# A graph layer's two sums put into one stage, with maxima, tally and stores of counts in the first sum's pass

## What is computed

```
_spmm(edge_src, edge_dst, edge_val, dense):
    msgs = dense[edge_src] * edge_val[:, None]
    return segment_sum(msgs, edge_dst, num_segments=N_NODES)

h1  = relu(_spmm(src, dst, edge_weight, y) @ W1 + b1)     # y: x after a normalization
out = elu (_spmm(src, dst, edge_weight, h1) @ W2 + b2)
x   = x + out
```

## Time and profile before

| | us |
|---|---|
| median of three runs | 3237.06 (3233.52 to 3242.03) |
| the profiled execution | 3245.63 |
| its span, first to last instruction | 3243.9 |
| first-sum stage, from its first transfer's issue | 451.7 to 838 |
| second-sum stage | 838 to 1171 |

### The profile page before, as it was taken

One profiled execution on the slowest core, in us unless ns is written; L12 is line 12 of the kernel. 1 busy time (PEld: TensorE's weight loads), 2 busy tenths in 40 slices (PEclk: granted clock), 3 DMA queues, 4 the chain that ended last, 5 costly groups with the idle time before them and its releaser, 6 DMA issues. The chain is left out here.

```text
span 3243.9 us, 43530 instructions
## 1 busy us (share of the span) xinstructions
PE 2517.5 (78%) x12901; PEld 1753.2 (54%) x12902; DVE 1539.5 (47%) x5059; ACT 1086.5 (33%) x2512; POOL 1714.6 (53%) x1286
## 2 busy tenths in 40 slices
PE   3344449799999975758979859599797999959991
PEld 1122224358544464646858645387596454549881
DVE  8899963354544553246553452543434000162326
ACT  6899940000243431124433312333344000012223
POOL 5888878885388123667848511386383300024443
PEclk9999999899999966978989855599798999959996
DMA  9999987688899824555536522454122544139994
GB/s 330 288 284 283 285 251 213 165 260 235 309 374 364 292 77 155 166 168 133 116 82 123 100 66 51 131 122 84 33 1 32 179 125 138 45 116 320 338 323 144
DMA packets 452978, 592.13 MB, mean 183 GB/s; under 512 B 166720, under 2 KB 357314, under 8 KB 442933
## 3 DMA queue, kind: packets, MB, share of 16 engines
q1 hardware_dynamic: 299670, 526.93, 47.6%
q0 software_dynamic: 127920, 42.48, 12.4%
q10 hardware_dynamic: 25200, 20.49, 1.9%
HBM read 413.49 MB, written 176.26 MB: 182 GB/s over the span
## 5 line engine op out<-in xcount | busy, mean ns | idle before, releaser
L659 POOL DMA_INDIRECT table_pairs<-sums,index_to x392 | 607.2, 1549 | 162.6 <-issue 118.9
L659 POOL DMA_INDIRECT table_t<-sums,index_from x392 | 619.7, 1581 | 118.9 <-issue 118.6
L981 PE MATMUL sum_psum<-abuf,y 128*128 128x512 f32 (+3 forms) x1800 | 568.9, 473 | 62.1 <-DMA abuf<-table_pairs 44.0
L981 PEld LDWEIGHTS sum_psum<-abuf,y 128*128 128x128 f32 x1800 | 297.1, 191 | 307.2 <-issue 251.1
L1398 PE MATMUL sum_psum<-wide,parts 128*128 128x512 f32 x1800 | 432.1, 394 | 7.3 <-DVE parts L1434 3.0
L1398 PEld LDWEIGHTS sum_psum<-wide,parts 128*128 128x128 f32 x1800 | 341.4, 190 | 81.2 <-DVE parts L1434 3.9
L981 PE MATMUL sum_psum<-abuf,acc 128*128 128x512 f32 (+1 forms) x700 | 293.0, 582 | 5.4 <-DMA abuf<-table_pairs 5.4
L533 PE MATMUL merge_psum<-part,acc 128*128 128x6 bf16 x980 | 71.0, 167 | 240.9 <-DVE pass_on L607 159.0
L1260 ACT ACTIVATE wide<-abuf 128x512 fp32r<-128x512 f16 (+1 forms) x264 | 148.5, 573 | 249.2 <-PE sum_psum L1398 225.6
L533 PEld LDWEIGHTS merge_psum<-part,acc 128*128 128x128 bf16 x980 | 56.8, 104 | 324.1 <-issue 321.7
L2085 ACT ACTIVATE m_x_h<-m_x_hp,m_x_b1t 128x128 f32<-128x128 f32 x374 | 109.3, 367 | 359.1 <-PE m_x_hp L2056 227.8
(11 more groups left out here) (478 smaller groups left out, 4145.4 us busy)
## 6 DMA issues: line engine op xcount, KB each, us to landing
abuf<-table_pairs SPq DMA_DIRECT2D x250, 512.0 KB
table_pairs<-zero SPq DMA_DIRECT2D x50, 1600.0 KB
abuf<-table_counts SPq DMA_DIRECT2D x90, 640.0 KB
table_t<-zero SPq DMA_DIRECT2D x25, 1600.0 KB
abuf<-table_t SPq DMA_DIRECT2D x150, 256.0 KB, 2.6
m_x_wa<-in_L_ffn_w_dram SPq DMA_DIRECT2D x65, 512.0 KB
m_x_wb<-in_L_ffn_w_dram SPq DMA_DIRECT2D x65, 512.0 KB
abuf<-table_pairs SPq DMA_DIRECT2D x150, 128.0 KB
```

What stands on the lines that cost most here:

```text
L659: nc.gpsimd.indirect_dma_start(table[:, :], bass.IndirectOffsetOnAxis(ap=index[:, g, j:j + 1], axis=0), k.sums[:, g, j, 0:width], None, co ...
L981: mm = nc.tensor.matmul(k.sum_psum[:, b % 2, f, lo:lo + n], h[:, c, f * P:(f + 1) * P], operand(i % ring, c - q * QUART, n), start=(c == 0 ...
```

## The change

Both sums stand in one stage, a new function `graph_layer`, without the barrier between them.

- `PIECES` is gone: `LIMITS` is 7, and each block waits for its whole bound.
- The first pass does, for each tile, the first sum on PE, the maximum and the tally on DVE (`count`), the cast and the store of counts on ACT. The GRU programs stay beside blocks 2 and 3. A slot of the ring (now 10, `RING_BOTH`) is free when PE, DVE (both steps) and ACT are done with it.
- The second pass loads all tiles again and does only the second sum on PE; a block's sums are now copied to SBUF by DVE (`join`), and the projection of a block stands after 3 tiles of the next, not 5.
- The choice of rare rows follows the first pass. Their gathers stand in POOL's program behind 10, 12, 14 and 16 lines of the transposed table (`RARE_AT`). DVE's program has `rare_rest_dve` of block 0 ahead of the first `join`.
- `some(13)` becomes `some(19)`, so 3 lines instead of 9 are left for the pooled stage.
- Both weight matrices are loaded at the start. The GRU's buffers lie in parts of others. Rare rows are stored by DMAs of their own.

```diff
-PIECES = {BLOCKS - 3: ((0, 2 * P), (2 * P, 2 * P)), BLOCKS - 2: tuple((j * P, P) for j in range(SPAN))}
-STARTS = [(b, lo) for b in range(BLOCKS) for lo, _ in PIECES.get(b, ((0, CUT),))]
-LIMITS = len(STARTS)
+LIMITS = BLOCKS
+RING_BOTH = 10
+RARE_AT = {10: (0, 1), 12: (2,), 14: (3, 4), 16: (5, 6)}
...
 def spread_edges(...):
-        if beside is not None:
-            beside(pool, 0)
-            beside(pool, 1)
         for g in range(first, first + lines):
...
-            if beside is not None and g > first and (g - first) % 3 == 0:
-                beside(pool, 1 + (g - first) // 3)
+            if beside is not None:
+                for b in RARE_AT.get(g - first, ()):
+                    beside(pool, b)
...
+def graph_layer(nc, k, block, name, table, *, h, weights, rows, loads, landed, peel, tally, tally_psum, partial,
+                aside):
...
+    @block.sync
+    def _(sp):
...
+        for i, (b, c) in enumerate(visits):
...
+            if i < len(first) and i % TILES == 0:
+                if b < BLOCKS - 1:
+                    needed = sp.value_load(k.bound[0:1, b:b + 1], min_val=16 * UNIT, max_val=16 * UNIT * LINES)
+                for half in range(2):
+                    sp.wait_ge(landed[half], needed if b < BLOCKS - 1 else 16 * UNIT * LINES)
+            if i >= ring:
+                sp.wait_ge(s["used"], i - ring + 1)
+                if i - ring < len(first):
+                    sp.wait_ge(s["tallied"], i - ring + 1)
+                    sp.wait_ge(s["peaked"], i - ring + 1)
+                    sp.wait_ge(s["cast"], i - ring + 1)
...
+    @block.scalar
+    def _(act):
...
+        def rare_rows(b):
+            own, n = slice(RARE, P), columns(b)
+            rare_narrow_act(nc, k, act, peel, b)
+            act.wait_ge(peel.rare_ready, b + 1)
...
+        act.wait_ge(peel.own_column, 1)
+        rare_rows(0)
+        for b in blocks:
+            raise_rows(b)
+            for r in (2 * b + 1, 2 * b + 2):
+                if r < BLOCKS:
+                    rare_rows(r)
...
+    @block.tensor
+    def _(pe):
...
+        for i, (b, c) in enumerate(first):
+            q = i % TILES
+            pe.wait_ge(loaded[i % ring], 16 * (i // ring + 1))
+            if q == 0 and b >= 2:
+                pe.wait_ge(s["evacuated"], KD * (b - 1))
+            mm = add(i, b % 2, h, q == 0, q == TILES - 1)
+            mm.then_inc(s["used"], 1)
...
+            if q + 1 == AHEAD and b:
+                project(b - 1)
+        for i, (b, c) in enumerate(second, len(first)):
...
+            if b == 0:
+                pe.wait_ge(s["known"], c + 1)
+            add(i, at, x1, q == 0, c == TILES - 1).then_inc(s["used"], 1)
+            if q == 2:
+                project(BLOCKS - 1 + b)
+            if b == 0 and q == AHEAD:
+                rare_ranks_pe(nc, k, pe, peel)
+            if b == 0 and q == 3 * AHEAD:
+                rare_names_pe(nc, k, pe, peel)
+        project(2 * BLOCKS - 1)
...
+        def count(i):
...
+            nc.vector.tensor_reduce(k.peaks[:, b, c:c + 1], got, AX_X, ALU.max).then_inc(s["peaked"], 1)
...
+                nc.vector.tensor_tensor(to, to, got, ALU.add).then_inc(s["tallied"], 1)
...
+        rare_flags_dve(nc, k, dve, link, peel)
+        for t in tiles_of(BLOCKS - 1):
+            know(t)
+        grade(BLOCKS - 1)
+        rare_index_dve(nc, k, dve, link, peel)
+        rare_rest_dve(nc, k, dve, peel, 0)
+        for b in blocks:
+            join(b)
+            for t in tiles_of(b):
+                take(t)
+                if t:
+                    close(t - 1)
+            for r in (2 * b + 1, 2 * b + 2):
+                if r < BLOCKS:
+                    rare_rest_dve(nc, k, dve, peel, r)
+        close(TILES - 1)
...
-        layer("l0a", pairs, "relu", k.y, weight_in=a["L0_gnn_W1"], rows_in=(a["L0_gnn_b1"],), out=k.acc,
...
-        reuse_semaphores()
-        layer("l0b", pairs, "elu", k.acc, weight_in=a["L0_gnn_W2"], rows_in=(a["L0_gnn_b2"],), which=0, tally=True, peel=True,
-              ring=RING_PEEL, meanwhile=some(13))
+            with nc.Block() as block:
+                graph_layer(nc, k, block, "l0", pairs, h=k.y, weights=weights, rows=(rows[:, 0, :], rows[:, 1, :]),
...
+                spread_edges(nc, k, block, pairs_laid, pairs, k.index_to, 2, BUILT, LINES - BUILT, last=True)
+                some(19)(block, lambda pool, b: rare_gather(nc, k, pool, peel, b))
```

More of the change, by code:

```diff
@@ L436, in _ @@
         link(nc.vector.tensor_reduce(k.bound_f[:, LIMITS:LIMITS + 1], high, AX_X, ALU.max))
-        for j, (b, lo) in enumerate(STARTS):
-            width = dict(PIECES.get(b, ((0, CUT),)))[lo]
-            nc.vector.memset(k.limit[:, j:j + 1], float(b * CUT + lo + width)).then_inc(link_sem, 1)
+        for b in range(BLOCKS):
+            nc.vector.memset(k.limit[:, b:b + 1], float((b + 1) * CUT)).then_inc(link_sem, 1)
         link.n += LIMITS
@@ L661, in _ @@
                         k.sums[:, g, j, 0:width], None, compute_op=ALU.add).then_inc(laid[half], 16)
-        if beside is not None:
-            for b in range(2 + (lines - 1) // 3, BLOCKS):
-                beside(pool, b)
         if last:
@@ L1124, in rare_rows_dve @@
     before, total, named = peel.psum[:, 0:TILES], peel.psum[:, 32:32 + TILES], peel.psum[:, 64:66]
-    link(nc.vector.tensor_reduce(top, k.peaks[:].rearrange("p b t -> p t b"), AX_X, ALU.max))
-    nc.vector.tensor_scalar(flag, top, float(EXACT), None, ALU.is_gt).then_inc(peel.flagged, 1)
     dve.wait_ge(peel.flagged, 1)
@@ L2917, in half @@
                     meanwhile(block)
-        layer("l0a", pairs, "relu", k.y, weight_in=a["L0_gnn_W1"], rows_in=(a["L0_gnn_b1"],), out=k.acc,
-              which=0, landed=pairs_laid, ring=RING_BESIDE, peaks=k.peaks, cuts=PIECES,
-              aside=[(2 + n, (f"gru{n}", *(a[f"L1_gnn_{v}{n}"] for v in ("iw", "wih", "whh", "bih", "bhh")), w[:]))
-                     for n, w in enumerate((k.gru0, k.gru1))],
-              meanwhile=lambda block: spread_edges(nc, k, block, pairs_laid, pairs, k.index_to, 2, BUILT, LINES - BUILT,
-                                                   last=True))
@@ L2925, in build @@
-        reuse_semaphores()
-        layer("l0b", pairs, "elu", k.acc, weight_in=a["L0_gnn_W2"], rows_in=(a["L0_gnn_b2"],), which=0, tally=True, peel=True,
-              ring=RING_PEEL, meanwhile=some(13))
+        with ExitStack() as scope:
+            k.abuf = held(scope, "abuf", [P, RING_BOTH, CUT, 2])
+            k.gathered = held(scope, "gathered", [P, 2, KD, CUT])
+            weights = [held(scope, f"weight{j}", [P, KD, D]) for j in range(2)]
+            rows = held(scope, "rows", [P, 2, D])
+            tally = held(scope, "tally", [P, 2, CUT])
+            partial = held(scope, "partial", [P, KD * (NP - CUT)])
+            late = held(scope, "late", [P, 12 * D])
+            k.sum_psum = bank(scope, "sum_psum", [P, 2, KD, 512])
+            k.out_psum = bank(scope, "out_psum", [P, 2, 512])
+            gates = bank(scope, "gru_bank", [P, 2, 512])
+            k.turn, k.shifted = (late[:, (8 + 2 * j) * D:(10 + 2 * j) * D].rearrange("p (t n) -> p t n", t=2) for j in range(2))
+            peel = Peel(nc, k, scope, counts, pairs, held(scope, "peeled", [P, PEELED, CUT], FP16),
+                        late[:, 0:8 * D].rearrange("p (u n a) -> p u n a", u=2, a=2), held(scope, "rare_rest", [P, NP], FP16),
+                        held(scope, "rare_narrow", [P, 2, CUT], FP16), held(scope, "rare_i", [P, BLOCKS], I32), gates[:, 0, :])
+            g = Gru(k.acc[:, 3 * SPAN:6 * SPAN, :], partial[:, 3 * KD * CUT:5 * KD * CUT], held(scope, "gru_ht", [P, KD, D]),
+                    late, gates)
+            programs = []
+            for n, w in enumerate((k.gru0, k.gru1)):
+                programs.append(gru_layer(nc, k, g, programs[-1] if n else None, f"gru{n}",
+                                          *(a[f"L1_gnn_{v}{n}"] for v in ("iw", "wih", "whh", "bih", "bhh")), w[:]))
+            with nc.Block() as block:
+                graph_layer(nc, k, block, "l0", pairs, h=k.y, weights=weights, rows=(rows[:, 0, :], rows[:, 1, :]),
+                            loads=[(weights[0][:], rows_of(a["L0_gnn_W1"], KD)), (weights[1][:], rows_of(a["L0_gnn_W2"], KD)),
+                                   (rows[:, 0, :], spread(a["L0_gnn_b1"])), (rows[:, 1, :], spread(a["L0_gnn_b2"]))],
+                            landed=pairs_laid, peel=peel, tally=tally, tally_psum=gates[:, 1, :],
+                            partial=partial,
+                            aside=[(2 + n, program) for n, program in enumerate(programs)])
+                spread_edges(nc, k, block, pairs_laid, pairs, k.index_to, 2, BUILT, LINES - BUILT, last=True)
+                some(19)(block, lambda pool, b: rare_gather(nc, k, pool, peel, b))
```

212 lines of the change are left out of this document (195 added, 17 removed).

## The result

| | before | changed | predicted |
|---|---|---|---|
| median, us | 3238.83 (4 runs, 3233.52 to 3242.03) | 3295.12 (4 runs, 3289.47 to 3299.97) | 3281, range 3255 to 3301 |
| ratio | 1 | 1.0175, interval 1.0153 to 1.0197 | 1.0136 |
| profiled execution | 3245.63 | 3294.74 (span 3293.0) | 3290 |
| first router matmul, end of the layer | 1173.47 | 1229.19 | 1217.5 |

The kernel became slower by 56.3 us; 44 were predicted. The layer's end, the first matmul of the router that follows it, moved by 55.7 us, so all of the loss lies in the changed stage. The first sum's stage starts at the same time in both.

A forecast was written before the change was run, and what follows sets the result against it. PE was taken to bound both sums, at 1.81 us a tile in the second. A shift of 49.3 us from the late join, less 4.9 of tally products, gave +44 on 3237.1: 3281 us, range 3255 to 3301.

The forecast's parts named there:

- Point 1: First sum without pieces: block 4 starts at 725.6 us, block 5 at 787 plus 3 for POOL's slower pace, ending at 841.5.
- Point 2: First pass: tally, cast and store cost nothing under PE's 1.81 us a tile; second pass starts at 858, 17 us later.
- Point 3: POOL beside stores: pair table full 3 us later (bounds 0 and 8), then 80 DMAs in 151 us, rare gather at 937.7.
- Point 4: Second pass, block 0's join: it ends at 944.5, PE idles 33 us at the projection, plus 3 us of half clock.
- Point 5: Rest of second pass: same 1.81 us a tile, tally products leave (-4.9 us), no second wait; +44 us at stage's end.
- Point 6: Pooled stage and elsewhere: POOL loses 48 DMAs, 89 us, none on the path; fewer bounds and a weight load below 1 us.
- The join's wait was paid: Denies the rival that rare rows come ahead of PE, leaving only the late start: +8.5 us, 3246; chance 0.08.
- load-pace rival: Second pass runs at the pace of loads, 1.40 us a tile, not 1.81: -6 us, 3231; chance 0.07.
- The first pass did not starve: Denies the rival that casts waiting for stores hold the ring; at 3.9 us a tile +20 us, 3301; chance 0.05.

## Why the prediction came out right, point by point

*Point 1, no pieces.* Right in kind, late by 13 us. Block 4's sum started at 736.5 (725.6 was forecast), block 5's at 802.8 (790 with the slowed pace). Of the second 12.8 us, some 10.8 are POOL's pace: its last pair DMA was over at 795.3 (issued at 793.7), not at 784.5. The other 2 are the landing, 7.6 us from there to PE's start, not 5.4.

*Point 2, tally, cast and store cost nothing.* Right for PE: within blocks there is no wait for them, and block 6 took 18 us up to the second pass, where 16.5 were forecast. But the step priced the add only by VectorE's own time. What it cost was POOL's time. The second pass started at 873.5, not 858, and PE stood at the join at 928.3, not 911.6.

*Point 3, POOL.* **This is the term that was mis-sized.** The text took the gathers' spacing of 1.92 us in the second sum, ascribed it to stores, and scaled it down to +3 us, bounds 0 and 8. The last pair DMA, due to be over by 781.5 without a slow-down, was over at 795.3, so +13.8 and not +3, outside the bounds too. The table was full and landed at 799.2, not 786.5, and the 80 DMAs behind it took 156.6 us, not 151. The gather came at 955.8, 18.1 late. The runs showed in place of the stores the adds of the tally, each of which holds up a DMA issued inside it. The same adds ran in the second sum before, so the 1.92 was a trace of them: 25 of 104 DMAs took above 1.6 us there, with 1.43 us of adds beside them, against 0.38 beside the rest.

*Point 4, what waits.* Right. Forecast: 33 us of idle at the joined projection, released by VectorE's copy; measured: 34.64 us. Both ends had moved by about the same (16.7 and 18.4 us), so the wait hardly shows the error. The row's cast began 4.4 us behind its issue, where 4 were taken for the landing. The clock behind the wait cost 3.1 us (the joined projection took 6.74 us, 3.67 before), where 3 were taken.

*Point 5, behind it.* No second wait, and no tally products behind the join, as forecast. Not forecast: the last block's narrow products, which took 15.18 us for 80 rows before, took 9.93 for 88. The row of before, in the same view:

```profile
1150.34 15.18 PE L981 MATMUL sum_psum<-abuf,acc 128*128 128x53 f32 x80
```

and its window, with the changed kernel's behind it, show the clock (the column ahead of the last two):

```profile
1150.00:1174.00 24.00, 18.35 (x93) 16.80 (x92) 13.73 (x49) 9.60 (x28) 0.00 (x0) 0.56 0.21 52
```

```profile
1206.00:1230.00 24.00, 16.93 (x124) 14.90 (x122) 13.03 (x42) 3.37 (x6) 0.00 (x0) 0.90 0.30 91
```

0.56 against 0.90. At the new pace the 80 rows would take 9.0 us, so that gave back 6.2 us; the last projection, in the same windows, took 1.07 us instead of 1.95 and gave back 0.9 more. The sum, corrected: 44 + 18.4 (join) - 6.2 - 0.9 = 55.3, against 55.7 measured.

*Point 6, elsewhere.* Right: POOL ended its DMAs in the pooled stage at 2426 us, and PE's products of that stage took 215 us from first to last, 216 before. Behind the layer's end the two profiled executions differ by under 7 us, within what the executions of one kernel differ by.

*The rivals.* None came. The join's wait was paid. The load-pace rival falls by PE's timeline of the second pass, with no stores of counts beside it:

```profile
887.76 18.25 PE L1245 MATMUL sum_psum<-abuf,acc 128*128 128x512 f32 x40
...
906.47 21.85 PE L1245 MATMUL sum_psum<-abuf,acc 128*128 128x512 f32 x48
```

18.25/40 and 21.85/48 are 0.456 us a product, 1.82 us a tile, where that rival needed under 1.45. The PEld share of the second pass is 0.42 (146 of 353 us), and PE was the bound all the same. So the share of weight loads, by which the Trainium skill (Perfetto Trace Analysis, section Identifying the Most-Contended Engine) would judge PE's headroom, misleads here when read alone. The section names beside it the share of peak arithmetic, which the prediction did not work out. The first pass did not starve.

That the total came within 14 us of the forecast owes something to chance: of the error of 18 us at the join, 7 us were paid back behind it by a higher clock that nobody had counted. Without them the sum gives 3299, just inside the range.

## What to carry to other kernels

When an indirect load stands in the middle of a long row of DMAs on POOL, work out when POOL gets to it before anything else; here a change to one table was worth 40 us, and letting the first join past its late row returned less than half of that (12 us, or 17 with the late entry taken off), since the next gather was late too. Price an operation that is moved beside another engine not only by its own time but by what it does to that engine: for VectorE beside POOL's DMAs, count the operations with two operands in SBUF and, by the few cases here, the copies from SBUF to SBUF. Where a gate leaves PE idle, look for products that need the same loaded tile; that gained more than undoing the change.

## What the runs showed of the hardware

- POOL's indirect DMA took 1.55 us beside VectorE's maxima without a gap. Issued while VectorE ran an add with two operands in SBUF, it ended 1.42 us behind the end of the add (32 of 36), and so took up to 2.09 us; beside a 3.49 us operation of this kind it took 4.12. The adds and maxima themselves kept their 0.68 us in the median: POOL alone paid.
- The granted clock of one stage can halve without any effect: 0.52 against 1.00 over the first 451 us, at equal length, since PE was not the bound there.
- Short waits cost more than their length: around gates of 11 to 16 us the mean granted clock of the 30 us shown fell to 0.78 to 0.83, and 20 products took 11.1 to 12.0 us, not 9.05.
